# A decoder layer's attention stage: fills on VectorE, another load order, spike steps of three operations, the last spikes in two halves

## The chip, the cores and the metric

The kernel runs on one core of one Trainium2 chip. The metric is the device time of one execution in microseconds. The kernel before was timed three times: 2955.64, 2957.96 and 2958.58 us, median 2957.96 us.

## The reference, cut to what matters

For 8 batches of 512 tokens by 256 features the layer computes three residual blocks: a two-way Mamba block with a feed-forward part, cross attention over a context, and a spiking feed-forward block.

```python
x = x + mamba_block(layernorm(x))                    # selective scan forwards and backwards, then a GELU feed-forward
x = x + cross_attention(layernorm(x), ctx, ctx, mask)  # 16 heads of 16; scores where mask == 0 are set to -1e9
h = square(relu(layernorm(x) @ W_fc.T))              # 256 -> 1024
y = h @ W_proj.T                                     # 1024 -> 256
mem = 0
for _ in range(5):                                   # BETA = 0.9, THRESHOLD = 1.0
    reset = mem > THRESHOLD
    mem = BETA * mem + y - reset * THRESHOLD
    count += mem > THRESHOLD
x = x + count / 5
```

## The kernel before, in words

There are two passes. `mamba_pass` runs the scans for all batches and stores its result in DRAM (`mid`). `attention_pass` does everything else, after every engine has waited for the semaphore `handover`. The change touches only the second pass.

The attention pass works on one batch of 512 tokens at a time. Tokens lie on 128 partitions in four tiles, so a tile of tokens by features is 128x1024 f32. The order on each engine is written out by hand, engine by engine, with semaphores between the engines; nothing is planned by a program. Each engine has a head (the work of batch 0 that must be there before the loop), then a loop over batches 0 to 6 whose body also prepares batch b+1, and the last batch, which prepares nothing.

Inside a batch TensorE first does pre-scores (`prescore`, queries by keys, 4 matmuls a head, of which VectorE takes row maxima, line 1775) mixed with the first feed-forward of the next batch, then scores, weighted values, the output projection, and the spiking feed-forward (`spike_input`). Queries and keys are cut into three bf16 parts on ScalarE and VectorE (`high`, `middle`, `cut_lo` at line 1668, `cut_last` at line 1672). SyncE's function `stacks(n, beta)` writes the parts to DRAM and reads them back six times into `k_st` (n = 0) or `q_st` (n = 1) in another layout: three writes and six reads of 256 KB each. Each read is issued only when the three writes have landed. The first `prescore` waits until both stacks are there.

The head, by engine:

- SyncE issues loads: x, the rows of biases, context 0, attention weights, the transposed mask, the mask (`mask_i`), the spiking block's second weights (`w_proj`), then x and the Mamba result for batch 1, `stacks(0, 0)`, context 1, `stacks(1, 0)`, and the spiking block's first weights (`w_fc`).
- TensorE finishes the first feed-forward of batch 0 (`down`, 64 matmuls), then projects keys and values, transposes the normalised queries' input `xn_q` and projects the queries.
- VectorE adds the feed-forward's result (`add_down`, line 1664), takes statistics, applies the norm to `xn_q` (line 1642, four operations of 128x256), cuts the keys, takes values (line 1678) and queries (line 1686), normalises the input of batch 1 (`first_norm(1)`, line 1642 again, tile `xn`), makes `mask_bias` from `mask_i`, and zeroes two tiles.
- GpSimd adds x and the Mamba result and a row (`start_x1n`, lines 1858 and 1860), makes the reciprocal deviation (`rstd_of`), fills constants in `k_st` and `v_sb` (lines 1887 to 1891), and adds another row (`take_x1`, line 1867).

The fills are a row of ones for the masking columns of the keys, zeros in the padding of the values and a column of ones there. Their four lines on GpSimd stand between `rstd_of(ATT, 0)` and `take_x1(0)`.

The spikes are computed on VectorE by `spikes(beta)`: `start`, `step(1)` to `step(4)` and `finish`. `start` has two comparisons, a step has a multiply-add, a subtraction, a count and (but for the last) a comparison, and `finish` has one operation. Inside a batch these steps stand between other work: the spikes of batch b-1 are computed while TensorE does the scores of batch b. Only the spikes of batch 7 stand alone, after everything else, and are followed by one store of 512 KB.

Of the kernel before, what the change touches and what calls it, by code (L numbers as in the profile page):

```python
# [22 lines left out]
QR = 6 * DH + 3  # L23
# [3 lines left out]
STEPS, BETA, THRESHOLD = 5, 0.9, 1.0  # L27
# [131 lines left out]
BEFORE, AFTER = "before", "after"  # L159
# [944 lines left out]
def attention_pass(nc, ctx, a, mid, out, sb, where, stage, psum, consts, handover, early):  # L1104

    f32, bf16, i32 = mybir.dt.float32, mybir.dt.bfloat16, mybir.dt.int32
    ALU, ACT, AX = mybir.AluOpType, mybir.ActivationFunctionType, mybir.AxisListType
    ident, cols, minus_half, col, settle, s_const = consts
    pair, bank, y_bank, general = psum
    KB = 1024  # L1110
# [34 lines left out]
    g0 = sb("g0", [P, T], f32, where["pr"] + 16 * KB)  # L1145
    masked = sb("masked", [P, 2, T], f32, where["pr"] + 20 * KB)

    mem, spk, cnt, tmp = (sb(name, [P, TT, D], f32, where["qk"] + 4 * KB * n)
                          for n, name in enumerate(("mem", "spk", "cnt", "tmp")))

    mask_i = sb("mask_i", [P, TT, T], i32, where["w_up1"])
    maskT_i = sb("maskT_i", [P, TT, T], i32, where["q_st"])
# [25 lines left out]
    s_mw = stage("max_write_dma", 16)  # L1178
    s_mr = [stage(f"max_read_dma{i}", 16) for i in range(2)]
    s_out = stage("out_dma", 16, ahead=16)  # L1180
    setup_dve = stage("setup2_dve")
    setup_pe = stage("setup2_pe")
    FF1, ATT, FF2 = range(3)
# [17 lines left out]
    with nc.Block() as block:  # L1201
# [4 lines left out]
        def _(sp):  # L1206
# [32 lines left out]
            def store(beta, slot):  # L1239
                sp.wait_ge(out_ready.sem, out_ready.count(beta))  # L1240
                settle(sp)
                dma(s_out, out[bass.ds(slot * TT, TT)].rearrange("j p f -> p j f"), tmp[:, :, :])

            def m_rows(b):

                for i in range(2):
                    heads = slice(i * H // 2, (i + 1) * H // 2)
                    sp.wait_ge(m_cut.sem, m_cut.count(2 * b + i))
                    dma(s_mw, m_dram[:, heads].rearrange("s h t -> h s t"), m_part[:, i])
                    sp.wait_ge(s_mw.sem, s_mw.count(2 * b + i))  # L1250
                    dma(s_mr[i], q_st[6 * DH:QR, heads, :], m_dram[:, heads])
# [5 lines left out]
            dma(s_att, w_att[:, :, :, :].rearrange("p w k e -> p (w k) e"),  # L1257
                a["w_att"].rearrange("w (k p) e -> p (w k) e", p=P))
            dma(s_maskT, maskT_i[:, :, :], a["maskT"].rearrange("(j p) t -> p j t", p=P))
            dma(s_mask, mask_i[:, :, :], a["mask"].rearrange("(j p) t -> p j t", p=P))  # L1260
            dma(s_ffw, w_down[1][:, :, :], a["w_proj"].rearrange("(k p) e -> p k e", p=P))
            sp.wait_ge(early.mid.sem, early.mid.count(B))
            x_used(0)
            load_x(1)
            stacks(0, 0)
            sp.wait_ge(*G.full(("v", 1), BEFORE))
            load_ctx(1)
            stacks(1, 0)
            sp.wait_ge(setup_dve.sem, setup_dve.count(1))
            dma(s_ffw, w_up[1][:, :, :], a["w_fc"].rearrange("(k p) e -> p k e", p=P))  # L1270
            with sp.Fori(0, B - 1) as b:
# [10 lines left out]
            m_rows(B - 1)  # L1282
            store(B - 1, B - 2)
            sp.wait_ge(s_out.sem, s_out.count(B - 1))
            store(B, B - 1)
            sp.wait_ge(s_out.sem, s_out.count(B))
            sp.wait_ge(s_x.sem, s_x.count(B))
            sp.wait_ge(s_ctx.sem, s_ctx.count(B))

# [327 lines left out]
        def _(dve):  # L1617
# [28 lines left out]
            def two(ap, jj):  # L1646
                return ap[:, 2 * jj:2 * jj + 2, :]

            def bank_tiles(bk):
                return bk[:, :].rearrange("p (j f) -> p j f", j=2)  # L1650
# [49 lines left out]
                                             rsum[:, j, :].unsqueeze(2).broadcast_to((P, 4, DH)), ALU.mult)  # L1700
                last.then_inc(G.done_sem(("ot", g)), 1)

            def spikes(beta):


                def start():
                    dve.wait_ge(s_out.sem, s_out.count(beta - 1))
                    settle(dve)
                    dve.drain()
                    dve.tensor_scalar(spk[A3], y_sb[A3], THRESHOLD, None, ALU.is_gt)  # L1710
                    dve.tensor_scalar(cnt[A3], y_sb[A3], THRESHOLD, None, ALU.is_gt)

                def step(i):
                    prev = y_sb if i == 1 else mem
                    dve.drain()
                    dve.scalar_tensor_tensor(tmp[A3], prev[A3], BETA, y_sb[A3], ALU.mult, ALU.add)
                    dve.drain()
                    dve.tensor_tensor(mem[A3], tmp[A3], spk[A3], ALU.subtract)
                    dve.drain()
                    dve.scalar_tensor_tensor(cnt[A3], mem[A3], THRESHOLD, cnt[A3], ALU.is_gt, ALU.add)  # L1720
                    if i < STEPS - 1:
                        dve.tensor_scalar(spk[A3], mem[A3], THRESHOLD, None, ALU.is_gt)

                def finish():
                    dve.drain()
                    dve.scalar_tensor_tensor(tmp[A3], cnt[A3], 1.0 / STEPS, x_res[A3], ALU.mult, ALU.add).then_inc(out_ready.sem, 1)
                return start, step, finish

            dve.memset(ones_bf[:, :], 1.0)
            dve.tensor_copy(ident_bf[:, :], ident[:, :])  # L1730
            dve.wait_ge(s_w.sem, s_w.count(0))
            add_down(0, BEFORE)
            norm_stats(ATT, x1n)
# [80 lines left out]
                    dve.wait_ge(*G.done(("fn", KD - 1), it))  # L1814
                    first_norm(b + 2)

            def take_y(it):
                for jj in range(TT // 2):
                    key = ("pr", jj)
                    dve.wait_ge(*G.full(key, it))  # L1820
                    bk = G.bank(key, it)
                    dve.tensor_copy(two(y_sb, jj), bank_tiles(bk)).then_inc(G.done_sem(key), 1)

            batch(0, 0, True)
            with dve.Fori(0, B - 2) as n:
                take_y(n)
                batch(n + 1, n + 1, True)
            take_y(B - 2)
            batch(B - 1, AFTER, False)
            take_y(AFTER)  # L1830
            start, step, finish = spikes(B)
            start()
            for i in range(1, STEPS):
                step(i)
            finish()


        @block.gpsimd
        def _(pool):
# [44 lines left out]
            pool.wait_ge(s_w.sem, s_w.count(0))  # L1884
            start_x1n(0)
            rstd_of(ATT, 0)
            pool.memset(k_st[6 * DH:QR, :, :], 1.0)
            pool.drain()
            pool.memset(v_sb[:, :, :, DH:32], 0.0)
            pool.drain()  # L1890
            pool.memset(v_sb[:, :, :, DH:DH + 1], 1.0).then_inc(s_v.sem, 1)
            pool.drain()
            take_x1(0)
            rstd_of(FF1, 1)

            def batch(b, more):
                if more:
# [141 lines left out]
```

## Time and profile before

| | us |
|---|---|
| runs (3) | 2955.64, 2957.96, 2958.58 |
| median | 2957.96 |
| the profiled execution's own time | 2953.11 |
| its span | 2951.3 |
| TensorE busy | 2742.2 (93%) |
| VectorE busy | 2215.5 (75%) |
| ScalarE busy | 1760.7 (60%) |
| GpSimd busy | 1559.6 (53%) |

The span is the time between the first and the last recorded work; the execution's own time is 1.8 us more. The attention pass starts at about 1704 us of the span, its first pre-score at 1775.72 us, and the last matmul ends at 2927 us. In the profile a row gives the engine, the source line, the operation and the tile that it writes and reads; many operations share the line of a helper, so that the tiles' names tell them apart. SPq is SyncE's queue of DMA issues, and a DMA's row there is the issue, not the transfer.

### The profile page before, as it was taken

To read this page: it belongs to the slowest core of one execution; us is meant where nothing else is said; L and a number is where in the kernel's file an instruction comes from. 1 tells how busy PE (TensorE), PEld (TensorE's weight loads), DVE (VectorE), ACT (ScalarE), POOL (GpSimd) and SP (SyncE) were. 2 spreads that over 40 slices of the span, in tenths; PEclk is the share of its full clock that TensorE was granted. 3 is DMA by queue.
4 is the path that set the end of the run, shared out by engine and by line. 5 is a ranking of instruction groups with operands and counts; after the bars stand their busy time and mean duration, and the time that the engine had idled before them with its cause. 6 is when DMAs were issued, how large, how long until landed. Compare 5 with 4: busy or idle time off the path is not lost. (4 is left out here: it accounts for less than half of the span.)

```text
span 2951.3 us, 55361 instructions
## 1 busy us (share of the span) xinstructions
PE 2742.2 (93%) x19289; PEld 1814.1 (61%) x19330; DVE 2215.5 (75%) x3289; ACT 1760.7 (60%) x2899; POOL 1559.6 (53%) x853
## 2 busy tenths in 40 slices
PE   5999999999999999999999849999999999999995
PEld 2777777777777777777777634445454545454423
DVE  3988888888888888888888757484848484747463
ACT  5778777877877787778777413534444444444341
POOL 1888888888888888888889631111111111111010
PEclk9999999999999999999999979999999999999988
DMA  3122212212121222122113071414050505050500
GB/s 115 33 72 76 68 53 70 88 33 80 68 76 41 72 76 69 52 75 83 36 64 101 1 164 35 68 27 72 23 77 18 93 2 93 2 93 2 78 9 8
DMA packets 113338, 174.50 MB, mean 59 GB/s; under 512 B 15216, under 2 KB 88048, under 8 KB 113040
## 3 DMA queue, kind: packets, MB, share of 16 engines
q1 hardware_dynamic: 113088, 171.34, 22.7%
q8 instruction: 136, 2.23, 0.3%
q14 instruction: 114, 0.93, 0.1%
HBM read 148.38 MB, written 22.94 MB: 58 GB/s over the span
## 5 line engine op out<-in xcount | busy, mean ns | idle before, releaser
L1066 POOL TENSOR_TENSOR hC<-h,C_rep 128x1024 f32<-128x1024 f32 x512 | 1204.3, 2367 | 235.3 <-PE y_bank L538 230.5
L924 DVE TENSOR_TENSOR_SCAN h<-dA,pair 128x512 f32<-128x512 f32 x1024 | 1178.5, 1204 | 159.1 <-PE pair L447 145.1
L677 ACT ACTIVATE dA<-delta,cols 128x511 f32<-128x511 f32 x1024 | 666.0, 712 | 98.3 <-DVE h L924 93.1
L447 PEld LDWEIGHTS pair<-diagB,duT 64*128 64x128 f32 x8192 | 497.9, 187 | 236.0 <-issue 185.0
L447 PE MATMUL pair<-diagB,duT 64*128 64x128 f32 x8192 | 595.9, 285 | 17.6 <-DVE h L924 8.8
L538 PE MATMUL y_bank<-ident,hC 128*128 128x128 f32 x4120 | 563.3, 280 | 13.7 <-POOL hC L1066 11.8
L538 PEld LDWEIGHTS y_bank<-ident,hC 128*128 128x128 f32 x4120 | 441.9, 141 | 79.9 <-POOL hC L1066 19.7
L1775 DVE CUSTOM_DVE_ANT_0 masked<-pair,mask_bias 128x512 f32<-128x512 f32 x512 | 322.0, 687 | 30.7 <-PE pair L1296 15.0
L1846 POOL TENSOR_SCALAR rstd<-mv 128x4 f32<-128x4 f32 x24 | 11.7, 486 | 567.8 <-DVE mv L1635 567.8
L1528 ACT ACTIVATE pr<-pair 128x1024 f32<-128x1024 f32 x256 | 248.7, 1022 | 94.0 <-PE pair L1296 83.7
L447 PE MATMUL general<-xnT,w_in 128*128 128x512 f32 x512 | 251.8, 603 | 7.4 <-ACT zs L677 5.2
L1875 POOL CAST m_part<-m_rest 8x512 bf16<-8x512 f32 x16 | 12.7, 792 | 421.3 <-ACT m_rest L1528 421.3
L1296 PE MATMUL general<-w_down,g 128*128 128x256 f32 x1024 | 232.5, 380 | 2.9 <-DVEq L1620 2.9
L1296 PEld LDWEIGHTS general<-w_down,g 128*128 128x128 f32 x1024 | 193.7, 190 | 35.0 <-issue 3.8
L1296 PE MATMUL pair<-q_st,k_st 99*128 99x512 bf16 x512 | 196.7, 384 | 13.3 <-ACT pr L1528 10.7
L1296 PE MATMUL general<-xT,w_up 128*128 128x512 f32 x360 | 184.5, 654 | 5.8 <-ACT xT L1528 5.5
L1296 PE MATMUL pair<-mask_biasT,ident_bf 128*128 128x512 bf16 x472 | 179.9, 381 | 0.0
L1296 PE MATMUL pair<-k_st,q_st 96*128 96x512 bf16 x512 | 151.1, 404 | 17.9 <-DMA q_st<-qk_parts 15.2
L934 DVE SCALAR_TENSOR_TENSOR u<-general,cols,u 128x511 f32<-128x511 f32 (+2 forms) x192 | 141.1, 735 | 26.1 <-ACT u L677 22.6
L1296 PEld LDWEIGHTS pair<-q_st,k_st 99*128 99x128 bf16 x512 | 50.2, 98 | 143.5 <-ACT pr L1528 97.7
L1695 DVE RECIPROCAL rsum<-general 128x16 f32<-128x16 f32 x32 | 8.3, 258 | 167.7 <-PE general L1428 167.7
L677 ACT ACTIVATE diagB<-eye,BT 128x64 f32<-128x64 f32 x512 | 127.6, 344 | 0.0
(174 smaller groups left out, 3146.1 us busy)
## 6 DMA issues: line engine op xcount, KB each, us to landing
C_rep<-c_rows SPq DMA_DIRECT2D x128, 512.0 KB, 3.7
w_in<-w_in SPq DMA_DIRECT2D x16, 1024.0 KB, 4.9
qk_parts<-qk_part SPq DMA_DIRECT2D x48, 256.0 KB, 2.5
k_st<-qk_parts SPq DMA_DIRECT2D x48, 256.0 KB, 8.8
q_st<-qk_parts SPq DMA_DIRECT2D x48, 256.0 KB, 8.9
x_in<-x SPq DMA_DIRECT2D x18, 512.0 KB, 5.4
w_out<-w_out SPq DMA_DIRECT2D x17, 512.0 KB, 4.3
mid<-x_out SPq DMA_DIRECT2D x9, 512.0 KB, 6.4
```

Source lines behind the costliest of these rows:

```text
L447: return pe.matmul(o, lhsT, rhs, start=start, stop=stop)
L538: last = pe.matmul(y_bank[:, c * P:(c + 1) * P], hC[:, g % 2, i, c * P:(c + 1) * P], ident[:, :], start=j == 0 and i == 0 and c == 0, stop ...
L677: return act.activation(o, i, fn, **kw)
L924: last = dve.tensor_tensor_scan(h[:, g % 4, i, :], dA[:, g % 4, i, :], dBu[:, i, :], 0.0, ALU.mult, ALU.add)
L934: dve.scalar_tensor_tensor(u[n][:, k, lag:T], raw[:, 0:T - lag], col("fb"[n] + "conv_w", CW * k + CW - 1 - lag), u[n][:, k, lag:T], ALU.mu ...
L1066: pool.tensor_tensor(hC[:, g % 2], h[:, g % 4], C_rep[:, 2 * j:2 * j + 2, :], ALU.mult).then_inc(s_hC.sem, 1)
L1296: return pe.matmul(o, lhsT, rhs, start=start, stop=stop)
L1528: return act.activation(o, i, fn, **kw)
L1695: dve.reciprocal(rsum[:, :, :], o[:, :, :, DH:DH + 1].squeeze(3))
L1775: dve.tensor_tensor_reduce(masked[:, j % 2, :], bank[j], mask_bias[:, j, :], 1.0, FLOOR, ALU.add, ALU.max, m_col[:, j, hd:hd + 1]).then_in ...
L1846: pool.tensor_scalar(rstd[:, :], mv[:, :, 1], EPS, None, ALU.add)
L1875: pool.tensor_copy(high, m_rest[:, :])
```

## The change

It has four parts.

1. The fills of `k_st` and `v_sb` go from GpSimd to the head of VectorE's block, ahead of `add_down`. On GpSimd `rstd_of(FF1, 1)` now comes before `take_x1(0)`.
2. In SyncE's head, `mask_i` is loaded after x of batch 1; `stacks(1, 0)` follows `stacks(0, 0)` directly; context 1 and `w_proj` are loaded after both.
3. A spike step has three operations: `mem` is kept negated, and the comparison of the reset is fused with the subtraction. The tile `spk` is gone, and `start` has one comparison.
4. The spikes of the last batch are done for tokens' tiles 0 and 1 first, right after their half of the projection has been copied, then for tiles 2 and 3; each half has its own store of 256 KB.

```diff
@@ sync
+            def store_half(jj):
+                sp.wait_ge(out_ready.sem, out_ready.count(B + jj))
+                two = slice(2 * jj, 2 * jj + 2)
+                dma(s_last, out[(B - 1) * TT + 2 * jj:(B - 1) * TT + 2 * jj + 2].rearrange("j p f -> p j f"), tmp[:, two, :])
@@
-            dma(s_mask, mask_i[:, :, :], a["mask"].rearrange("(j p) t -> p j t", p=P))
-            dma(s_ffw, w_down[1][:, :, :], a["w_proj"].rearrange("(k p) e -> p k e", p=P))
             sp.wait_ge(early.mid.sem, early.mid.count(B))
             x_used(0)
             load_x(1)
+            dma(s_mask, mask_i[:, :, :], a["mask"].rearrange("(j p) t -> p j t", p=P))
             stacks(0, 0)
+            stacks(1, 0)
             sp.wait_ge(*G.full(("v", 1), BEFORE))
             load_ctx(1)
-            stacks(1, 0)
+            dma(s_ffw, w_down[1][:, :, :], a["w_proj"].rearrange("(k p) e -> p k e", p=P))
             sp.wait_ge(setup_dve.sem, setup_dve.count(1))
             dma(s_ffw, w_up[1][:, :, :], a["w_fc"].rearrange("(k p) e -> p k e", p=P))
@@
-            store(B, B - 1)
-            sp.wait_ge(s_out.sem, s_out.count(B))
+            for jj in range(TT // 2):
+                store_half(jj)
+            sp.wait_ge(s_last.sem, s_last.count(0))
@@ vector
-            def spikes(beta):
+            def spikes(beta, cols_of=(A3,)):
                 def start():
...
-                    dve.tensor_scalar(spk[A3], y_sb[A3], THRESHOLD, None, ALU.is_gt)
-                    dve.tensor_scalar(cnt[A3], y_sb[A3], THRESHOLD, None, ALU.is_gt)
+                    for c in cols_of:
+                        dve.tensor_scalar(cnt[c], y_sb[c], THRESHOLD, None, ALU.is_gt)
                 def step(i):
-                    prev = y_sb if i == 1 else mem
-                    dve.drain()
-                    dve.scalar_tensor_tensor(tmp[A3], prev[A3], BETA, y_sb[A3], ALU.mult, ALU.add)
-                    dve.drain()
-                    dve.tensor_tensor(mem[A3], tmp[A3], spk[A3], ALU.subtract)
-                    dve.drain()
-                    dve.scalar_tensor_tensor(cnt[A3], mem[A3], THRESHOLD, cnt[A3], ALU.is_gt, ALU.add)
-                    if i < STEPS - 1:
-                        dve.tensor_scalar(spk[A3], mem[A3], THRESHOLD, None, ALU.is_gt)
+                    for c in cols_of:
+                        dve.drain()
+                        if i == 1:
+                            dve.scalar_tensor_tensor(tmp[c], y_sb[c], BETA, y_sb[c], ALU.mult, ALU.add)
+                            dve.drain()
+                            dve.scalar_tensor_tensor(mem[c], y_sb[c], THRESHOLD, tmp[c], ALU.is_gt, ALU.subtract)
+                        else:
+                            dve.scalar_tensor_tensor(tmp[c], mem[c], -BETA, y_sb[c], ALU.mult, ALU.add)
+                            dve.drain()
+                            dve.scalar_tensor_tensor(mem[c], mem[c], -THRESHOLD, tmp[c], ALU.is_lt, ALU.subtract)
+                        dve.drain()
+                        dve.scalar_tensor_tensor(cnt[c], mem[c], -THRESHOLD, cnt[c], ALU.is_lt, ALU.add)
@@
             dve.tensor_copy(ident_bf[:, :], ident[:, :])
+            dve.memset(k_st[6 * DH:QR, :, :], 1.0)
+            dve.memset(v_sb[:, :, :, DH:32], 0.0)
+            dve.drain()
+            dve.memset(v_sb[:, :, :, DH:DH + 1], 1.0).then_inc(s_v.sem, 1)
             dve.wait_ge(s_w.sem, s_w.count(0))
             add_down(0, BEFORE)
@@
             batch(B - 1, AFTER, False)
-            take_y(AFTER)
-            start, step, finish = spikes(B)
-            start()
-            for i in range(1, STEPS):
-                step(i)
-            finish()
+            for jj in range(TT // 2):
+                take_y(AFTER, jj)
+                start, step, finish = spikes(B, ((slice(None), slice(2 * jj, 2 * jj + 2), slice(None)),))
+                start()
+                for i in range(1, STEPS):
+                    step(i)
+                finish()
@@ gpsimd
             rstd_of(ATT, 0)
-            pool.memset(k_st[6 * DH:QR, :, :], 1.0)
-            pool.drain()
-            pool.memset(v_sb[:, :, :, DH:32], 0.0)
-            pool.drain()
-            pool.memset(v_sb[:, :, :, DH:DH + 1], 1.0).then_inc(s_v.sem, 1)
-            pool.drain()
+            rstd_of(FF1, 1)
             take_x1(0)
-            rstd_of(FF1, 1)
```

`take_y` now takes one half (`jj`); its other callers loop over both halves as before.

## Rows read from the trace of the kernel before

**Rows 1.** Windows: engines' busy us (count), clock, DMA share, GB/s; head and a loop batch.

```profile
1704.00:1776.00 72.00, 31.82 (x116) 22.61 (x118) 42.69 (x49) 10.70 (x12) 23.17 (x12) 0.73 0.82 180
1922.00:2068.00 146.00, 139.54 (x619) 72.86 (x623) 93.16 (x217) 64.27 (x80) 20.84 (x17) 0.98 0.29 50
```

**Rows 2.** Chain that ended last, over the head: start us, us, what.

```profile
1704.66 14.07 PE general L1296 x64
...
1723.80 8.88 DVE xn_q L1642 x4
1732.68 3.29 DVE qk L1668
...
1751.89 8.72 DMA qk_parts<-qk_part
...
1762.96 12.63 DMA q_st<-qk_parts
```

**Rows 3.** Timeline of GpSimd in the head: start us, us, instruction.

```profile
1712.87 2.35 POOL L1860 TENSOR_TENSOR x1n<-x1n,rows 128x1024 f32<-128x1024 f32 x1
...
1723.90 6.92 POOL L1887 MEMSET k_st<- 3x8192 bf16 x1
...
1732.47 2.41 POOL L1867 TENSOR_TENSOR x<-x1n,rows 128x1024 f32<-128x1024 f32 x1 [0.26 <-issue]
```

**Rows 4.** Timeline of VectorE, in the head and in the loop's second batch.

```profile
1718.74 0.69 DVE L1664 TENSOR_TENSOR x1n<-x1n,general 128x512 f32<-128x512 f32 x1 [2.75 <-PE general L1296]
...
1754.53 5.66 DVE L1642 TENSOR_SCALAR xn<-x_mid,mv,rstd 128x256 f32<-128x256 f32 x4 [1.64 <-POOL rstd L1848]
...
1776.51 0.69 DVE L1775 CUSTOM_DVE_ANT_0 masked<-pair,mask_bias 128x512 f32<-128x512 f32 x1 [7.26 <-issue]
...
1979.45 1.38 DVE L1642 TENSOR_SCALAR xn_q<-x1n,mv,rstd 128x256 f32<-128x256 f32 x4 [1.65 <-POOL rstd L1848]
...
2031.36 3.44 DVE L1642 TENSOR_SCALAR xn<-x_res,mv,rstd 128x256 f32<-128x256 f32 x4 [1.31 <-POOL rstd L1848]
...
2043.68 1.23 DVE L1668 TENSOR_TENSOR qk<-qk,qk_part 128x1024 f32<-128x1024 f32 x1 [6.97 <-ACT qk_part L1528]
```

**Rows 5.** Groups of fills on VectorE, shapes apart: line, shape, count, busy us, mean ns.

```profile
L982 DVE MEMSET u<- 128x2048 f32 x1 | 1.8, 1765 | 0.4 <-issue 0.4
...
L1729 DVE MEMSET ones_bf<- 128x128 bf16 x1 | 0.2, 165 | 2.5 <-PEq L312 2.5
```

**Rows 6.** Timeline of SyncE's DMA issues in the head.

```profile
1742.55 2.97 SPq L1211 DMA_DIRECT2D k_st<-qk_parts  x6
1745.56 0.45 SPq L1211 DMA_DIRECT2D ctxT<-ctxT  x1
```

**Rows 7.** Windows of the head, columns as in rows 1.

```profile
1742.80:1756.50 13.70, 2.64 (x5) 0.73 (x3) 7.71 (x14) 3.40 (x3) 2.87 (x3) 0.75 1.08 123
1756.50:1760.50 4.00, 0.17 (x1) 0.18 (x2) 3.91 (x4) 0.00 (x0) 3.08 (x2) 0.50 0.92 303
```

**Rows 8.** Waits in the loop: who for whom, us, times, longest (VectorE's; TensorE's).

```profile
DVE rsum L1695 <- PE general L1428: 20.2, 4, 6.4
...
PE pair L1296 <- DMA q_st<-qk_parts: 1.8, 2, 1.0
```

**Rows 9.** Timeline of VectorE and SyncE at the end.

```profile
2920.22 0.69 DVE L1822 COPY y_sb<-general 128x512 f32<-128x512 f32 x1 [25.43 <-PE general L1296]
2927.13 0.69 DVE L1822 COPY y_sb<-general 128x512 f32<-128x512 f32 x1 [6.22 <-PE general L1296]
2927.92 0.69 DVE L1710 TENSOR_SCALAR spk<-y_sb 128x1024 f32<-128x1024 f32 x1
...
2948.00 0.41 SPq L1211 DMA_DIRECT2D out<-tmp  x1
```

**Rows 10.** Groups of VectorE at the end, and a half-size operation of the first pass.

```profile
L1718 DVE TENSOR_TENSOR mem<-tmp,spk 128x1024 f32<-128x1024 f32 x4 | 4.9, 1226 | 0.3
L945 DVE SCALAR_TENSOR_TENSOR yT<-general,zs x65: 659/666/692, 83.5 to 1688.1; 128x512 f32<-128x512 f32 x65
```

More of the change, by code:

```diff
@@ L1146, in attention_pass @@
     masked = sb("masked", [P, 2, T], f32, where["pr"] + 20 * KB)
-    mem, spk, cnt, tmp = (sb(name, [P, TT, D], f32, where["qk"] + 4 * KB * n)
-                          for n, name in enumerate(("mem", "spk", "cnt", "tmp")))
+    mem, cnt, tmp = (sb(name, [P, TT, D], f32, where["qk"] + 4 * KB * n)
+                     for n, name in enumerate(("mem", "cnt", "tmp")))
     mask_i = sb("mask_i", [P, TT, T], i32, where["w_up1"])
@@ L1180, in attention_pass @@
     s_out = stage("out_dma", 16, ahead=16)
+    s_last = stage("last_out_dma", 32)
     setup_dve = stage("setup2_dve")
@@ L1709, in start @@
                     dve.drain()
-                    dve.tensor_scalar(spk[A3], y_sb[A3], THRESHOLD, None, ALU.is_gt)
-                    dve.tensor_scalar(cnt[A3], y_sb[A3], THRESHOLD, None, ALU.is_gt)
+                    for c in cols_of:
+                        dve.tensor_scalar(cnt[c], y_sb[c], THRESHOLD, None, ALU.is_gt)
                 def step(i):
-                    prev = y_sb if i == 1 else mem
-                    dve.drain()
-                    dve.scalar_tensor_tensor(tmp[A3], prev[A3], BETA, y_sb[A3], ALU.mult, ALU.add)
-                    dve.drain()
-                    dve.tensor_tensor(mem[A3], tmp[A3], spk[A3], ALU.subtract)
-                    dve.drain()
-                    dve.scalar_tensor_tensor(cnt[A3], mem[A3], THRESHOLD, cnt[A3], ALU.is_gt, ALU.add)
-                    if i < STEPS - 1:
-                        dve.tensor_scalar(spk[A3], mem[A3], THRESHOLD, None, ALU.is_gt)
+                    for c in cols_of:
[10 more added lines that the diff above has]
+                        dve.scalar_tensor_tensor(cnt[c], mem[c], -THRESHOLD, cnt[c], ALU.is_lt, ALU.add)
                 def finish():
                     dve.drain()
-                    dve.scalar_tensor_tensor(tmp[A3], cnt[A3], 1.0 / STEPS, x_res[A3], ALU.mult, ALU.add).then_inc(out_ready.sem, 1)
+                    for c in cols_of:
+                        dve.scalar_tensor_tensor(tmp[c], cnt[c], 1.0 / STEPS, x_res[c], ALU.mult, ALU.add).then_inc(out_ready.sem, 1)
                 return start, step, finish
@@ L1815, in batch, with take_y @@
                     first_norm(b + 2)
[L1817 to L1822, printed above, removed]
+            def take_y(it, jj):
+                key = ("pr", jj)
+                dve.wait_ge(*G.full(key, it))
+                bk = G.bank(key, it)
+                dve.tensor_copy(two(y_sb, jj), bank_tiles(bk)).then_inc(G.done_sem(key), 1)
             batch(0, 0, True)
             with dve.Fori(0, B - 2) as n:
-                take_y(n)
+                for jj in range(TT // 2):
+                    take_y(n, jj)
                 batch(n + 1, n + 1, True)
-            take_y(B - 2)
+            for jj in range(TT // 2):
+                take_y(B - 2, jj)
             batch(B - 1, AFTER, False)
-            take_y(AFTER)
-            start, step, finish = spikes(B)
-            start()
-            for i in range(1, STEPS):
-                step(i)
-            finish()
+            for jj in range(TT // 2):
+                take_y(AFTER, jj)
[4 more added lines that the diff above has]
+                finish()
         @block.gpsimd
```

## The prediction, made before the changed kernel was run

> **What bounds the kernel now.** I read the windows first, to see which stretches have room. In a loop batch TensorE is busy 139.5 of 146 us; in the head, from the handover to the first pre-score, only 31.8 of 72 us [rows 1]. Behind the last matmul it does nothing at all. So only the head and the end are bound by something other than TensorE, and the change touches both, besides the loop.
>
> Second, the chain that ended last, over the head [rows 2]. It goes through TensorE's 64 matmuls (14.07 us), then through VectorE's `xn_q` (8.88 us for four operations) and its `qk` (3.29), and later through two DMA waits, 8.72 us for the writes of the query parts and 12.63 for their last read into `q_st`. The reader should look at the two VectorE entries with suspicion. In a loop batch the same four `xn_q` operations take 1.38 us and the same `qk` operation 1.23 [rows 4].
>
> Third, GpSimd's timeline beside it [rows 3]. During `xn_q` GpSimd fills `k_st` for 6.92 us (1723.90 to 1730.82), and during `qk` it runs `take_x1` for 2.41 us. Four operations of this norm take 1.38 us alone, 3.44 where one GpSimd addition of some 2.35 us runs beside them, and 5.66 where two do [rows 4]. So each GpSimd operation that runs beside these VectorE operations costs about its own length, 2.1 to 2.2 us for an addition.
>
> Fourth, SyncE's issues [rows 6] and the traffic [rows 7]. The six reads into `k_st` are issued at 1742.55 and move at 123 GB/s until about 1756.5; then 303 GB/s flow until 1760.5. That is context 1 (issued at 1745.56, right behind the reads) and the query writes (issued from 1750.96), which queue behind the reads: transfers are served in the order of issue. The query writes were thus ready long before they could land, and what sets their landing is when the reads into `k_st` began, plus context 1.
>
> **Part 1, fills on VectorE.** On VectorE a fill of 2048 elements takes 1765 ns and one of 128 bf16 elements 165 ns [rows 5], so 0.833 ns an element and 0.06 fixed. The three fills (8192, 1024, 64 elements a partition) cost 6.88 + 0.91 + 0.11 = 7.9 us. VectorE is free from 1705.3, when its two small constants are done, and would be done at 1713.3. Its next work, the first half of `x1n`, waits for GpSimd until 1715.22 [rows 3], and the second half waits 2.75 us for TensorE until 1718.74 [rows 4]. So the fills are covered by GpSimd's two additions, with 2 us to spare, and by TensorE's matmuls with another 2.7. Cost: 0 (if the cover were gone, 7.9). If the fills also blocked GpSimd's additions entirely, `x1n` would begin at 1713.3 instead of 1710.4 and end at 1718.2; the first half would be added by 1718.9, which costs 0.2 us. Bounds: 0 to 0.5.
>
> What it gives: `xn_q` 8.88 to 1.38, 7.5 us. `take_x1` now waits behind `rstd_of(FF1, 1)`, whose statistics come some 20 us later, so `qk` goes from 3.37 (its row in full) to 1.23, 2.1 us. Together 9.6 us earlier for everything that VectorE does behind it: keys' parts, values, queries. I see nothing that takes over: ScalarE's cast of 1.06 us sits behind `qk` and beside two other VectorE operations (`keep`, `not_full`, 1.8 us), and TensorE's small count of the mask ends at about 1726.5 before VectorE wants it. Bounds 8.5 to 10.
>
> `take_x1` moves to stand beside `first_norm(1)`, where GpSimd already has two additions. From 1.38, 3.44, 5.66 for none, one and two [rows 4], three make about 7.9, so 2.2 us more. Queued behind it on VectorE are the mask's preparation and the first row maximum; VectorE idled 7.26 us before that one [rows 4].
>
> **Part 2, order of loads.** The reads into `k_st` are issued 9.6 us earlier, at about 1733, and end at about 1747. The query parts are ready 9.6 us earlier too (writes issued at about 1741.3), so their writes queue right behind the reads, without context 1 between. 512 KB at 303 GB/s, the mean of a window that is idle for a part, are 1.7 us; I take 1.5. So `q_st`'s reads are issued at 1760.63 - 9.6 - 1.5 = 1749.5 and the first pre-score starts at 1775.72 - 11.1 = 1764.6. The bounds on the 1.5 are 0 (the landing has a fixed part that hides it) and 2. The moved loads: `mask_i` is 1 MB behind x of batch 1 in a stretch where no stack is under way, and is wanted by VectorE only at about 1753; `w_proj` and context 1 come behind `q_st`'s reads and are wanted in the feed-forward and projections over 100 us later. SyncE waits for the stacks a little longer before it issues them, with nothing urgent behind. Cost 0, if transfers go on being served in order.
>
> What is late next: VectorE reaches `mask_bias` and its two zero fills 9.6 us earlier and 2.2 us later by the third addition, so its slack before the first row maximum is 7.26 - 11.1 + 9.6 - 2.2 = 3.6 us. It is not the bound. Head: -11.1 us, bounds -8 to -12.5 (the landing of `q_st` itself varies by a microsecond or so).
>
> **Part 3, three operations.** Each loop batch loses four comparisons (0.69 us each) on VectorE, 2.8 us. But there VectorE waits for TensorE before the four `rsum`, 20.2 us in a batch, and of TensorE's waits over six batches none is for a spike operation, and `q_st` has 1.8 us in all [rows 8]. The loop gains 0. The one new kind of operation (comparison fused with subtraction) has no row; the nearest are the plain subtraction of the same tiles, 1226 ns, and the count, which is a comparison fused with an addition and is as long. I take 1.23. In the loop it would have to be about 3 us longer before it ended the 5 to 6 us waits.
>
> **Part 4, last spikes in halves.** Before: the second copy at 2927.13, the spikes from 2927.92, the store at 2948.00 [rows 9]. After: the first half's spikes begin after the first copy, at 2920.22, beside TensorE's last matmuls. A half has a copy (0.79 to the next start), a comparison (0.42 + 0.07), twelve operations at 0.69 + 0.07 and a last one of 0.69: 11.1 us. The gap of 0.07 is the 0.3 us idle over four operations; 0.69 for 512 elements is the longest of the 659 to 692 ns of `yT` [rows 10]; with 1226 for 1024 this leaves a fixed part of 0.15 us, and so 0.42 for half of the comparison's 0.69 [rows 9]. Two halves end at 2920.22 + 22.2 = 2942.4, and the store is issued 5.5 us earlier than at 2948.00. Had an operation 0.61 (half of 1.226) or 0.75, 26 of them would shift it by 2 us down or 1.5 up. The first half's store is long under way. The last one has 256 KB instead of 512, 0.9 us less at 303 GB/s, of which I take 0.7 for the same reason (bounds 0 and 1.5). End: -6.2 us, bounds -4 to -9.
>
> The Trainium skill, "VectorE: DVE Perf Modes", section on the trn2 errata, speaks of a fixed extra latency per instruction and gives 58 cycles plus the element count at 0.96 GHz for SBUF sources, so that 512 elements would take 0.59 us (an estimate from that page) and the halves would end 2.5 us earlier still, a sum of -19.8. This trace disagrees on the size: 1024 elements take 1226 ns, not the 1127 of that formula, so halving an operation saves only 0.54 of 1.23. The sum goes by the row.
>
> **Sum.** -11.1 - 6.2 = -17.3 us. The profiled execution took 2953.11 us by its own time (span 2951.3), so it would take 2935.8. The median of the runs shown is 2957.96, 4.9 us above it; against that I expect 2940.7, and that is the time I give. A measurement of this kernel can tell about 0.2%, 5.9 us, from no change.
>
> **Rivals.**
> - The head gives less: the late loads share the engines with `q_st`'s reads. Context 1 and `w_proj` are 1.57 million bytes; at 303 GB/s they would push the last read by 5.2 us at most. For it: they are issued while the reads are under way. Against: the reads into `k_st` moved at 123 GB/s and the 303 came only behind them [rows 7]. Or VectorE's mask chain eats its 3.6 us of slack, and the same few microseconds go. Sum -12.1: 2945.9. Chance 0.13.
> - GpSimd's fills are not what lengthens `xn_q`. Then the head keeps only the 1.5 us of part 2, and -7.7 gives 2950.3. Against: `xn_q` ended at 1732.68, just as GpSimd turned from its fills to `take_x1` (1732.47), and 8.88 less 1.38 is about the length of the fills. Chance 0.05.
> - The loop gains too, 2.8 us in each of 8 batches, 22 us: 2918. Against: the waits of rows 8. Chance 0.03.
> - The loop gives back what the ends gain: another phase of transfers at each of seven boundaries makes `q_st` the last to arrive, as it is now in two [rows 8]; 2 us each would leave -3.3: 2954.7. Chance 0.03.
> - Slower: the fused comparison and subtraction runs much longer than 1.23 us. It is one in three of the step's operations and sits eight times on the end's path, so it decides from 17.3/8 = 2.2 us more for a half, 2.9 in all, four times the plain one; at 3.5 us the end alone costs 22.5 more, and before the first `rsum` of a loop batch two steps would lose their 4.9 us wait and a few more. That gives 2970. Against: the count is the same kind of operation with 1226 ns. Chance 0.03.
>
> **Numbers.** The forecast has 0.73. Range 2934 to 2948: below by the bounds of head and end, above by the first rival and the spread of three runs (3 us); outside stay 2 in 10. Faster by over 0.2%: 0.73 + 0.13 + 0.03 and 0.04 of the second rival, 0.93. Within 0.2%: 0.04. Slower: 0.03.
>
> **What would show it.** In the changed profile: VectorE's fills with 6.9 us ending by 1713.5 and `x1n` at 1718.7 as before; `xn_q` 1.4 us and the first `qk` 1.2; `xn` of batch 1 about 7.9; query writes that land by about 1749.5 and the first pre-score at about 1764.6; VectorE idle about 3.6 us before it; loop batches of 144 to 146 us as before; spike operations of the last batch at 0.69 from the first copy on, and 11.1 us from the last copy to the last store, where there were 20.9. The forecast is wrong if the first pre-score is later than 1768, if VectorE or a memory transfer stands right before it with another tile, if the period of a loop batch moves, or if the new operation is not as long as its neighbours.

## The result, and the profile after

The changed kernel takes 2938.12 us in the median of five runs (2934.87 to 2943.01), the kernel before 2956.8 us (2954.3 to 2958.58). The ratio is 0.9943 with a 95% interval of 0.9932 to 0.9955, so it is 0.57% faster. The forecast was 2940.7, range 2934 to 2948. The profiled execution took 2934.87 us (span 2933.1) where the sum said 2935.8.

The windows of the changed kernel, columns as in [rows 1], show the head 10 us shorter with the same work on TensorE, and a loop batch as before but for VectorE, which has five operations less in a window 2 us shorter:

```profile
1705.50:1766.00 60.50, 29.95 (x115) 21.56 (x116) 42.86 (x52) 10.70 (x12) 15.08 (x9) 0.74 0.88 181
2058.00:2202.00 144.00, 137.51 (x610) 71.47 (x616) 89.15 (x212) 63.59 (x79) 21.35 (x17) 0.99 0.28 50
```

The chain that ended last, over the head of the changed kernel, answers to [rows 2]. `xn_q` and the first `qk` have shrunk (8.88 to 1.38 us and 3.29 to 1.14), the two waits for transfers have hardly changed:

```profile
1705.52 14.06 PE general L1303 x64
...
1724.65 1.38 DVE xn_q L1649 x4
1726.04 1.14 DVE qk L1675
...
1742.61 8.71 DMA qk_parts<-qk_part
...
1753.67 12.24 DMA q_st<-qk_parts
```

VectorE's timeline in the changed kernel, against [rows 4] and [rows 5], with the fills now at its top:

```profile
1706.06 0.16 DVE L1741 CAST ident_bf<-ident 128x128 bf16<-128x128 f32 x1
1707.96 6.88 DVE L1742 MEMSET k_st<- 3x8192 bf16 x1 [1.75 <-issue]
1715.11 0.91 DVE L1743 MEMSET v_sb<- 128x1024 f32 x1 [0.26 <-issue]
1716.18 0.11 DVE L1745 MEMSET v_sb<- 128x64 f32 x1 [0.16 <-issue]
1716.29 0.69 DVE L1671 TENSOR_TENSOR x1n<-x1n,general 128x512 f32<-128x512 f32 x1
1719.61 0.69 DVE L1671 TENSOR_TENSOR x1n<-x1n,general 128x512 f32<-128x512 f32 x1 [2.63 <-PE general L1303]
...
1745.23 5.49 DVE L1649 TENSOR_SCALAR xn<-x_mid,mv,rstd 128x256 f32<-128x256 f32 x4 [1.64 <-POOL rstd L1865]
1750.82 3.33 DVE L1771 TENSOR_SCALAR keep<-mask_i 128x2048 f32<-128x2048 int32 x1
...
1766.84 0.69 DVE L1790 CUSTOM_DVE_ANT_0 masked<-pair,mask_bias 128x512 f32<-128x512 f32 x1 [4.96 <-issue]
```

GpSimd's timeline and SyncE's issues in the changed kernel, against [rows 3] and [rows 6]. The three additions stand together at the input norm of batch 1, and `q_st`'s reads are issued at 1751.34:

```profile
1713.83 2.36 POOL L1877 TENSOR_TENSOR x1n<-x1n,rows 128x1024 f32<-128x1024 f32 x1
...
1745.45 2.39 POOL L1884 TENSOR_TENSOR x<-x1n,rows 128x1024 f32<-128x1024 f32 x1 [0.25 <-issue]
1748.24 2.34 POOL L1875 TENSOR_TENSOR x1n<-x_in,x_mid 128x1024 f32<-128x1024 f32 x1 [0.40 <-issue]
1750.72 2.34 POOL L1877 TENSOR_TENSOR x1n<-x1n,rows 128x1024 f32<-128x1024 f32 x1
```

```profile
1733.74 2.97 SPq L1212 DMA_DIRECT2D k_st<-qk_parts  x6
1741.67 1.44 SPq L1212 DMA_DIRECT2D qk_parts<-qk_part  x3
1751.34 2.78 SPq L1212 DMA_DIRECT2D q_st<-qk_parts  x6
1754.16 0.45 SPq L1212 DMA_DIRECT2D ctxT<-ctxT  x1
1754.65 0.47 SPq L1212 DMA_DIRECT2D w_down<-w_proj  x1
```

The end of the changed kernel, against [rows 9] and [rows 10]. The second copy no longer stands at the arrival of its data but behind the first half's last operation. The fused operation (`mem<-y_sb,tmp`) is as long as its neighbours:

```profile
2907.92 0.69 DVE L1836 COPY y_sb<-general 128x512 f32<-128x512 f32 x1 [25.12 <-PE general L1303]
2908.70 0.43 DVE L1718 TENSOR_SCALAR cnt<-y_sb 128x512 f32<-128x512 f32 x1
2909.20 0.69 DVE L1724 SCALAR_TENSOR_TENSOR tmp<-y_sb 128x512 f32<-128x512 f32 x1
2909.97 0.69 DVE L1726 SCALAR_TENSOR_TENSOR mem<-y_sb,tmp 128x512 f32<-128x512 f32 x1
2910.74 0.69 DVE L1732 SCALAR_TENSOR_TENSOR cnt<-mem,cnt 128x512 f32<-128x512 f32 x1
...
2919.37 0.68 DVE L1836 COPY y_sb<-general 128x512 f32<-128x512 f32 x1
...
2929.84 0.69 DVE L1737 SCALAR_TENSOR_TENSOR tmp<-cnt,x_res 128x512 f32<-128x512 f32 x1
```

In the loop VectorE's shorter steps became longer waits for TensorE. In one batch (2068 to 2213 us before, 2058 to 2202 after) its waits ahead of `rsum` add up to 23.3 us, where they were 20.2 [rows 8]:

```profile
DVE rsum L1702 <- PE general L1435: 23.3, 4, 7.7
```

One execution against another differs by some microseconds in places that the change does not touch, so that the spans alone don't decide a term of 2 us. I therefore cut each profiled execution at eight points, all read from its timelines: the first down matmul; `x1n`'s second addition; the issue of `k_st`'s reads; of `q_st`'s reads; the first pre-score; the first pre-score of the last batch; the first of the last two copies; the end of VectorE's last operation. The table gives the stretches in us: "down" runs from the first of these points to the second, "to k reads" from the second to the third, and so on; "rest" runs from the last point to the end of the span. In e8 the fills and not the matmuls set "down", and in f1 and f2 the keys' projection is part of it.

| kernel | first matmul at | down | to k reads | to q reads | to pre-score | 7 batches | last batch | spikes | rest | span |
|---|---|---|---|---|---|---|---|---|---|---|
| before | 1704.66 | 14.08 | 23.81 | 18.08 | 15.09 | 1016.02 | 128.48 | 27.71 | 3.37 | 2951.3 |
| changed | 1705.52 | 14.09 | 14.13 | 17.60 | 14.71 | 1013.83 | 128.04 | 22.61 | 2.57 | 2933.1 |
| changed, again | 1706.68 | 17.13 | 14.14 | 16.95 | 15.67 | 1012.27 | 129.74 | 22.62 | 2.60 | 2937.8 |
| p1_fills | 1708.19 | 15.77 | 14.15 | 18.86 | 15.66 | 1010.84 | 128.45 | 27.70 | 3.38 | 2943.0 |
| p2_loads | 1704.98 | 14.09 | 23.79 | 17.41 | 15.43 | 1012.14 | 132.14 | 27.70 | 3.42 | 2951.1 |
| p3_steps | 1704.78 | 17.11 | 23.82 | 18.53 | 14.76 | 1013.41 | 131.70 | 25.29 | 3.40 | 2952.8 |
| p4_halves | 1707.95 | 14.09 | 23.80 | 18.83 | 15.24 | 1011.63 | 128.41 | 25.31 | 2.54 | 2947.8 |
| e5_fills_only | 1705.06 | 14.08 | 16.19 | 18.16 | 15.93 | 1013.04 | 128.34 | 27.70 | 3.40 | 2941.9 |
| e6_x1_only | 1707.02 | 15.77 | 21.64 | 17.91 | 14.33 | 1011.22 | 132.43 | 27.71 | 3.37 | 2951.4 |
| e7_ctx_between | 1706.77 | 15.78 | 14.13 | 19.45 | 16.38 | 1012.19 | 131.93 | 22.62 | 2.55 | 2941.8 |
| e8_double_fill | 1707.22 | 19.99 | 14.14 | 16.86 | 15.85 | 1010.00 | 132.50 | 22.60 | 2.54 | 2941.7 |
| f1_keys_first | 1707.63 | 19.06 | 7.45 | 17.81 | 15.15 | 1014.37 | 132.19 | 22.62 | 2.52 | 2938.8 |
| f2_act_copy | 1706.37 | 20.54 | 7.47 | 17.82 | 15.56 | 1011.13 | 129.82 | 22.01 | 2.58 | 2933.3 |

Before to changed, the 18.2 us of the two spans are: 0.9 more before the pass, 10.5 less in the head, 2.2 less in seven batches, 0.4 in the last, 5.1 in the spikes, 0.8 behind them.

### The profile page after: what moved, and what is told of

It is laid out like the page before. It is cut to its first block and busy times, and to the rows that moved or that the text cites. A ratio compares the mean times of both kernels' runs of the same rounds, so it can differ in the third digit from the quotient of the medians.

```text
span 2933.1 us, 55353 instructions
## 1 busy us (share of the span) xinstructions
PE 2739.0 (93%) x19289; PEld 1812.9 (62%) x19330; DVE 2189.3 (75%) x3270; ACT 1757.3 (60%) x2899; POOL 1554.4 (53%) x850
## 5 line engine op out<-in xcount | busy, mean ns | idle before, releaser
L447 PE MATMUL pair<-diagB,duT 64*128 64x128 f32 x8192 | 595.9, 285 | 17.9 <-issue 9.0
L1303 PE MATMUL pair<-q_st,k_st 99*128 99x512 bf16 x512 | 196.4, 384 | 13.6 <-ACT pr L1535 11.1
L1303 PE MATMUL pair<-k_st,q_st 96*128 96x512 bf16 x512 | 150.6, 403 | 17.3 <-DMA q_st<-qk_parts 13.7
L1303 PEld LDWEIGHTS general<-xT,w_up 128*128 128x128 f32 x360 | 74.1, 210 | 85.5 <-issue 74.8
```

The lines of the kernel that those rows point to most:

```text
L447: return pe.matmul(o, lhsT, rhs, start=start, stop=stop)
L1303: return pe.matmul(o, lhsT, rhs, start=start, stop=stop)
```

## The experiments

**The four parts, each alone on the kernel before.**

```diff
 # p1_fills (dve head; pool head)
+            dve.memset(k_st[6 * DH:QR, :, :], 1.0) ...
-            pool.memset(k_st[6 * DH:QR, :, :], 1.0) ...
-            take_x1(0)
             rstd_of(FF1, 1)
+            take_x1(0)
```

> Part 1 alone on the kernel before: fills on VectorE, take_x1 behind rstd_of(FF1, 1). My theory (each GpSimd operation beside xn_q and the first qk cost its own length): from the first down matmul to the issue of the k_st reads 9.6 us less (37.9 to 28.3), to the first pre-score about 9.6 less (71.1 to 61.5), nothing else moves: -9.6 us. Rival (fills are not what lengthens xn_q): xn_q stays near 8.9 us, 0 to -2 us in all.

Measured: ratio 0.9958 (0.9944 to 0.9972). The stretch to `k_st`'s reads is 14.15 us instead of 23.81, 9.7 less, where 9.6 was expected. It is the one part whose interval alone is clear of no change. To the first pre-score this profiled execution gained less than the 9.6 us expected, 6.6 (64.4 us from the first matmul, 71.1 before): its down matmuls took 1.7 us longer, for a reason that the control below shows, and the two stretches behind `k_st`'s reads 1.4 us.

```diff
 # p2_loads (sync head)
-            dma(s_mask, ...); dma(s_ffw, w_down[1] ...)
             load_x(1)
+            dma(s_mask, ...)
             stacks(0, 0)
+            stacks(1, 0)
             load_ctx(1)
-            stacks(1, 0)
+            dma(s_ffw, w_down[1] ...)
```

> Part 2 alone on the kernel before: the other load order. Prediction's term: context 1 no longer between k_st's reads and the query writes, 1.5 us earlier q_st, -1.5 us. Rival, from the changed kernel's profile, where the issue of q_st's reads came only 0.5 us earlier than VectorE's 9.7 explains: -0.5 us or nothing, because the landing of the writes is bounded by something else. A third: the later loads slow q_st's reads, 0 to +5 us.

Measured: ratio 0.9994 (0.9983 to 1.0005), which can't tell 1.5 us from nothing. From `k_st`'s reads to `q_st`'s 17.41 us instead of 18.08. Over all executions of the table that have context 1 between the stacks (before, p1, p3, p4, e5, e6, e7) this stretch is 17.9 to 19.5, mean 18.5; over the four that have it behind both and the keys as before (changed, again, p2, e8) 16.9 to 17.6, mean 17.2. The two groups do not overlap. So the part gives some 1.3 us of this stretch, near the 1.5 of the sum; the 0.5 of the first pair is one draw of a stretch that varies by 1.5 and 0.7 us within the two groups. The late loads do not slow `q_st`'s reads clearly: 14.7 to 15.9 us to the pre-score, mean 15.4, with both behind them (the same four), 14.3 to 15.9, mean 15.2, with neither (before, p1, p3, p4, e5, e6). The longest, 16.4, is e7, which has only `w_proj` behind them.

```diff
 # p3_steps: spikes with three operations, tile spk gone, whole tiles, one store; of the edit only this:
-                    dve.tensor_tensor(mem[A3], tmp[A3], spk[A3], ALU.subtract)
+                            dve.scalar_tensor_tensor(mem[c], mem[c], -THRESHOLD, tmp[c], ALU.is_lt, ALU.subtract)
```

> Part 3 alone on the kernel before: steps of three operations, whole tiles at the end, one store. My theory: the loop gives nothing; at the end four comparisons leave the chain, one of 0.61 to 0.69 in start and three of 0.60, so 20.1 us from the first comparison to the store become 17.7: -2.4 us. Rival (the 2.2 us by which batches 0 to 6 were shorter in the changed kernel came from the steps): -4.6 us, with the seven periods 2.2 us less in sum.

Measured: ratio 0.9999 (0.9989 to 1.0009). The spikes' stretch is 25.29 us, 2.4 less, as expected. The whole time can't show it: its interval reaches from 3.3 us less to 2.7 us more. In the profiled execution 3.0 us were lost in the down matmuls and 3.2 in the last batch. Its seven batches take 1013.4 us; p1, p2 and p4, which have the old steps, 1010.8, 1012.1 and 1011.6. The rival, that the loop gains by the steps, is refuted by both, since its 4.6 us in all lie outside the interval: the 2.2 us of the first pair were a long loop in the profiled execution of the kernel before.

```diff
 # p4_halves: for jj: take_y(AFTER, jj), spikes of that half, store_half(jj); steps of four operations
```

> Part 4 alone on the kernel before: the last spikes and the last store in two halves, with the old steps of four operations. My theory: 12.5 us a half (copy 0.79, comparisons 0.35 + 0.5, three steps of 2.28 + 0.35, one of 2.28, 0.69), so the last store is issued 25.0 us after the first copy instead of 27.8, and its landing is 0.8 us shorter: -3.6 us. Rival (a half has the full fixed cost, halving an operation saves less than 0.54 us): 0 to -1.

Measured: ratio 0.9991 (0.9982 to 1.0001). Spikes 25.31 us (2.4 less; expected 2.8), rest 2.54 us (0.8 less). So halves give 3.2 us. Parts 3 and 4 alone shorten the spikes by 2.4 us each, both together by 5.1, so they nearly add. So do the four ratios: alone the parts give 0.42, 0.06, 0.01 and 0.09%, in sum 0.58, and the changed kernel has 0.57.

**What lengthened `xn_q` and `qk`.** Two kernels split part 1.

```diff
 # e5_fills_only: fills on VectorE, on GpSimd still take_x1(0) ahead of rstd_of(FF1, 1)
 # e6_x1_only: fills on GpSimd, rstd_of(FF1, 1) ahead of take_x1(0)
```

> The kernel before with the fills on VectorE, but take_x1 on GpSimd still ahead of rstd_of(FF1, 1), so that it runs right behind rstd_of(ATT, 0). My theory: take_x1 (2.4 us) now stands beside xn_q instead of qk, so xn_q is about 3.4 us and qk 1.23, and the reads into k_st come 7.5 us earlier than before, 2.1 later than with part 1 whole: -7.5 us. Rival (the long xn_q has another cause): xn_q as in the kernel before.

> The kernel before with only the order of take_x1 and rstd_of(FF1, 1) turned round; the fills stay on GpSimd. My theory: xn_q stays 8.9 us, the first qk goes from 3.37 to 1.23 us, the first pre-score 2.1 us earlier: -2.1 us; xn of batch 1 and the mask's first operation together 2.2 us longer, hidden. Rival (the two parts are not additive, one wait hides the other): 0.

Measured: e5 0.9973 (0.9960 to 0.9986), e6 0.9991 (0.9978 to 1.0003). VectorE's and GpSimd's rows of e5, then VectorE's of e6:

```profile
1724.20 3.41 DVE L1642 TENSOR_SCALAR xn_q<-x1n,mv,rstd 128x256 f32<-128x256 f32 x4 [1.30 <-POOL rstd L1852]
1727.54 1.21 DVE L1668 TENSOR_TENSOR qk<-qk,qk_part 128x1024 f32<-128x1024 f32 x1
```

```profile
1724.42 2.40 POOL L1871 TENSOR_TENSOR x<-x1n,rows 128x1024 f32<-128x1024 f32 x1 [0.26 <-issue]
```

```profile
1727.84 8.88 DVE L1642 TENSOR_SCALAR xn_q<-x1n,mv,rstd 128x256 f32<-128x256 f32 x4 [1.30 <-POOL rstd L1848]
1736.64 1.21 DVE L1668 TENSOR_TENSOR qk<-qk,qk_part 128x1024 f32<-128x1024 f32 x1
```

With the fills gone and `take_x1` beside it `xn_q` is 3.41 us; with the fills beside it, 8.88. The stretch to `k_st`'s reads falls by 7.6 and 2.2 us (expected 7.5 and 2.1), and 7.6 + 2.2 is p1's 9.7 within 0.2. So both kinds of GpSimd work tried here, fills and an addition, cost these operations about their own length. The kernel before shows how, since its four `xn_q` operations are not evenly slow (shortest, median and longest in ns), and GpSimd's second fill stands beside the second of them:

```profile
L1642 DVE TENSOR_SCALAR xn_q<-x1n,mv,rstd x4: 394/776/7170, 1723.8 to 1732.3; 128x256 f32<-128x256 f32 x4
```

```profile
1730.94 0.96 POOL L1889 MEMSET v_sb<- 128x1024 f32 x1
```

The first operation takes 7.17 us, from 1723.80 to 1730.97, and the fill beside it ends at 1730.82 [rows 3]: one operation stood for as long as one fill ran. In e5, with the addition beside them, one of the four takes 2.44 us and the others about 0.40. Not every pair does this. In the changed kernel GpSimd's two additions (2.35 and 2.36 us) run beside VectorE's fill (6.88 us), and none of the three is longer than without the other.

**Context 1 between the stacks, in the changed kernel.**

```diff
 # e7_ctx_between
             sp.wait_ge(*G.full(("v", 1), BEFORE))
             load_ctx(1)
+            stacks(1, 0)
```

> The changed kernel, with context 1 loaded again between the two stacks (w_proj still behind them). Prediction's term: +1.5 us at the issue of q_st's reads and in the time. Rival (from the changed profile): +0.5 us or less, as the write's landing waits for something other than 512 KB of traffic.

Measured: 0.9952 (0.9940 to 0.9965) against before. The stretch is 19.45 us, 1.9 more than the changed kernel's 17.60 and 2.5 more than its repeat's 16.95. It lies on the side of the sum's term (1.5), not of the rival's 0.5. The whole time, beside 0.9943 and (in the control) 0.9952 for the changed kernel, can't tell them apart.

**How much cover the fills had.**

```diff
 # e8_double_fill
             dve.memset(k_st[6 * DH:QR, :, :], 1.0)
+            dve.drain()
+            dve.memset(k_st[6 * DH:QR, :, :], 1.0)
```

> The changed kernel, with the fill of k_st done twice on VectorE: 6.95 us more ahead of add_down. In the changed profile the fills end at 1716.3, just as GpSimd's x1n does, and TensorE's second half comes at 1719.6, so 2.6 us of cover are left: my theory is +4.3 us (fills end 1723.2, both additions follow back to back and end at 1724.6 instead of 1720.3), all of it at the first pre-score. Rival (the cover was the 10 us of the prediction, 2 + 2.7 us to spare beyond the fills): +2.2 us. Rival (k_st's stack is not on the path): 0.

Measured: 0.9956 (0.9942 to 0.9969). VectorE's rows:

```profile
1709.66 6.88 DVE L1742 MEMSET k_st<- 3x8192 bf16 x1 [1.75 <-issue]
1718.35 6.88 DVE L1744 MEMSET k_st<- 3x8192 bf16 x1 [1.80 <-issue]
1725.49 0.91 DVE L1745 MEMSET v_sb<- 128x1024 f32 x1 [0.26 <-issue]
1726.56 0.11 DVE L1747 MEMSET v_sb<- 128x64 f32 x1 [0.16 <-issue]
1726.61 1.28 DVE L1671 TENSOR_TENSOR x1n<-x1n,general 128x512 f32<-128x512 f32 x2
```

Two equal fills start 8.69 us apart though each row says 6.88. The row of a fill on VectorE is shorter than the fill, and the missing part stands as idle time ("issue") ahead of its own row: 1.75 and 1.80 us ahead of the two large fills, 0.26 and 0.16 ahead of the small ones. The doubled fill ends both additions 4.2 us later than in p1, e6 and e7, whose down matmuls took 15.8 us (20.7 against 16.5 us from the first matmul), and the issue of `k_st`'s reads also comes 4.2 us later (34.1 against 29.9). That agrees with the 4.3 expected, but for two errors that cancel: the fill was 8.7 us and not 6.95, and the additions of the undisturbed kernel came 1.7 us later than in the profile that the expectation used.

All of it reaches the first pre-score, as expected. The kernels to compare with are those with the same load order: from `k_st`'s reads to the pre-score it is 32.7 us here, 32.3 in the changed kernel and 32.6 in its repeat. So `k_st`'s reads are on the path, and the rival that they are not falls. The other rival (2.2 us) took the fill as the row has it and the cover as the prediction had it; it is 2 us off.

**A control and two further versions.**

> The changed kernel once more, as a control beside the next two. My theory of what varies between executions: the granted clock of TensorE in short stretches. The stages, counted from the first down matmul, should be: k_st's reads at 28.2 us (or later by as much as the down matmuls take longer than 14.1), first pre-score 32 to 32.5 us behind that, seven periods 1010 to 1014 us in sum, 22.6 us from the first of the last copies to the end of the last operation, 2.6 us behind it. In all 2935 to 2943 us.

Measured: 2942.05 us, 0.9952 (0.9939 to 0.9965), where the result had 0.9943. The stages came as expected: 32.6 us from `k_st`'s reads to the pre-score, 1012.3 for the seven periods, 22.62 and 2.60 at the end, and `k_st`'s reads 3.0 us late, just what the down matmuls took longer (17.13 us for 14.1). The granted clock goes with that, as windows over the first 14 us of these matmuls show (changed kernel, e6, p3; the clock is the third number from the end):

```profile
1705.52:1719.52 14.00, 14.00 (x65) 12.35 (x66) 8.84 (x6) 0.00 (x0) 4.71 (x2) 1.00 0.97 304
```

```profile
1707.02:1721.02 14.00, 14.00 (x57) 12.05 (x58) 0.93 (x3) 0.00 (x0) 4.68 (x2) 0.88 0.99 324
```

```profile
1704.78:1718.78 14.00, 14.00 (x51) 11.81 (x52) 0.93 (x3) 0.00 (x0) 4.70 (x2) 0.78 0.95 327
```

At a mean granted clock of 1.00, 0.88 and 0.78 the same matmuls take 14.1, 15.8 and 17.1 us; the repeat too had 0.78. The last batch, windowed from its first pre-score to the first copy, follows the clock in the same way: 128.0 to 128.5 us at 0.83 or 0.84 (before, changed, p1, p4, e5), 129.7 and 129.8 at 0.80 (the repeat, f2), 131.7 to 132.5 at 0.77 to 0.79 (the other six).

```diff
 # f1_keys_first, on the changed kernel
-            for step in range(2 * TT):
+            for step in range(2 * TT - 2):
                 down(step, BEFORE)
             ... project_k(0, m, BEFORE) ...
+            for step in range(2 * TT - 2, 2 * TT):
+                down(step, BEFORE)
 # VectorE: cut_lo(0, 0) between the two additions of add_down, cut_last(0, 0) right after norm_stats(ATT)
 # f2_act_copy, on f1: ScalarE copies the second half of the last y
```

> The changed kernel with the keys' stack made earlier: TensorE projects the keys before the last two of eight down steps, VectorE cuts the keys between the two additions and in the gap before the norm. My theory (k_st's reads hold up the query writes for some 7 us): k_st's reads issued 3 to 4.5 us earlier, the query parts ready 1.5 to 2.5 us later but still about when the reads end, q_st's reads and the first pre-score 2.5 to 4 us earlier: -3 us. Rival (the query chain takes over as bound, since the second addition comes 3.7 us later): 0 to +1.5 us.

> f1_keys_first, and ScalarE instead of VectorE copies the second half of the last projection while VectorE computes the first half's spikes. My theory (VectorE's chain sets the end, 22.6 us from the first copy): one copy and its gap of 0.77 us leave it, 21.8 us, -0.8 us on top of f1. Rival (ScalarE's copy comes late): 0.

Measured: f1 2936.7 us, 0.9933 (0.9920 to 0.9946); f2 2936.1 us, 0.9933 (0.9920 to 0.9945); the changed kernel in the same series 2942.05. Both medians lie below those of both other kernels, but the intervals of f1 and of the changed kernel (0.9939 to 0.9965) overlap, so a gain over the changed kernel is not shown by the times. In the profiled executions `q_st`'s reads are issued 44.3 us after the first matmul in f1 and 45.8 in f2, against 45.8 in the changed kernel and 48.2 in its repeat. The pair with the same granted clock over the first 14 us (0.78) is the repeat and f2: there `q_st`'s reads come 2.4 us earlier and the first pre-score 2.5 (61.4 for 63.9), at the lower end of the 2.5 to 4 expected.

`k_st`'s reads come only 1.7 us earlier in f1 than in the changed kernel (26.5 for 28.2), not 3 to 4.5, since this execution's second addition stands at 19.1 us, and the query parts are ready 4.5 us later (40.6 for 36.1), twice the expected. So the rival came true in part: the query chain is the bound in f1. There `q_st`'s reads follow the query writes by 3.7 us, as short a time as `k_st`'s reads follow the key writes in every execution of the table, where in the changed kernel it is 9.7 (in f2 4.7). VectorE in f1, at the end of the head:

```profile
1766.48 0.91 DVE L1784 MEMSET y_sb<- 128x1024 f32 x1 [0.34 <-issue]
1767.56 0.91 DVE L1785 MEMSET x_res<- 128x1024 f32 x1 [0.16 <-issue]
1768.38 0.63 DVE L1793 CUSTOM_DVE_ANT_0 masked<-pair,mask_bias 128x512 f32<-128x512 f32 x1
```

The idle time ahead of the first row maximum, 7.26 us before and 4.96 after the change, is gone in f1 and 0.81 us in f2: the mask behind the query chain now ends about together with `q_st`. f2 takes 0.6 us out of the spikes (22.01 for 22.62), of 0.8 expected.

## Why the prediction was right

**Where the loss was.** Right, and shown: e5 and e6 separate the fills (7.6 us) from `take_x1` (2.2), p1 has both (9.7); the sum had 7.5, 2.1 and 9.6. The rival with another cause falls. What makes VectorE's operation wait for GpSimd's wasn't tested, only that it does, for about the length of the GpSimd operation.

**Cover of the fills.** The cost of 0 came out, the working did not, and for the first addition that was luck. The step took 0.833 ns an element from the rows of fills; but the fills ended at 1716.29, 10.1 us behind the constants and not 7.9, and of the 2 us to spare nothing was left: GpSimd's `x1n` ends at 1716.19. The first addition starts 0.1 us behind it, as in the kernel before. Behind that there was still cover: the second half waits 2.63 us for TensorE. The evidence was in the rows of before: the fill of 2048 elements has 0.4 us of "issue" idle ahead of it [rows 5], and belongs to it.

**Later loads.** The term of 1.5 us came out at 1.3 in the mean and 0.5 in the first pair, a difference within the stretch's own spread. In that pair even the 0.5 can't be put down to context 1: the query writes came 0.5 us sooner behind `k_st`'s reads (7.9 for 8.4), and `q_st`'s reads 9.7 us behind these writes in both. The first rival, late loads that push `q_st`'s last read by up to 5.2 us, did not come: 0.2 us in the mean.

**The third addition beside the norm of batch 1.** The place was partly wrong, the size right: `xn` is 5.49 us, much as the 5.66 before, but the last of the three additions now stands beside the mask's first operation, which is 3.33 instead of 1.23, so 1.9 us more in sum where 2.2 was said. The slack before the first row maximum was 4.96 us instead of 3.6, as the first pre-score came 0.6 us later than forecast and VectorE 0.8 earlier.

**The head** gave 10.5 us of 11.1 in the profiled pair.

**The loop.** 0 fits: the seven batches take 1010.8 to 1013.0 us in the five experiments with the old steps and 1010.0 to 1014.4 in the seven executions with the new ones; only the execution before, with 1016.0, stands out. And the 2.8 us turned into waits of VectorE, 3.1 us more ahead of `rsum` in the batch shown.

**The end.** Two halves took 22.6 us for 22.2, one gap of 0.43 us between two operations being the difference; the fused operation took 0.69 us as assumed, so the slower rival never began. The store gave 0.8 us for 0.7. Together 5.9 for 6.2. The formula quoted from the Trainium skill, "VectorE: DVE Perf Modes", would have had 19.7 us for the halves; the measured 0.69 us, not 0.59, decides against it here. The same section of the Trainium skill remarks under its table that the measured fixed part is nearer 150 cycles than 58; with that an estimate gives 0.69 and 1.22 us for 512 and 1024 elements, and the trace's 0.69 and 1.226 agree.

**The sum.** -17.3 against -18.2 in the profiled pair, of which 2.2 came from the loop by chance and 0.9 went the other way ahead of the pass; head and end alone gave -16.4. So the closeness of the whole is partly luck, that of head and end is not. The ratios of result and control, 0.9943 and 0.9952, are -17 and -14 us.

## What to carry to other kernels

Look for operations that take longer in one place than the same form elsewhere, and read the other engine that shares their time: here 7.6 of 17 us were four small operations beside GpSimd's fills, and 2.2 more were one operation beside an addition. Before moving work under a cover, take its length from the starts of successive operations, with the idle time ahead of its row, and not from the row alone. And judge parts of 2 us by cutting the executions at common events, since the whole time varied by more than that.

## What the runs showed of the hardware that was not expected

A fill on VectorE occupies about 1.06 ns an element (8.69 us from start to start for 8192 in e8), while its row shows 0.84 (6.88 us); the same fill on GpSimd took 6.92 us, and GpSimd's next operation started 0.12 us behind it (1730.94).

A VectorE operation of the norm can stand for the whole of a GpSimd fill beside it (7.17 us, where the shortest of the four took 0.39), while a fill on VectorE and additions on GpSimd ran beside each other at full length (6.88, 2.35 and 2.36 us).

The granted clock over the same matmuls at the same place differed between executions, 1.00, 0.88 or 0.78, though TensorE had been busy for 7.2 of the 10 us before and for all of the 10 us before that in each of the three (in the one with 0.78 the clock was 0.96 in the last 10 us before, in the others 1.00).
